# A graph kernel whose first pass gets 16 extra products of constants in each slot

## The chip, the cores and the metric

The kernel runs on one core of a Trainium2 chip. The metric is the device time of one execution in microseconds. The kernel before took 4850.95 us in the median of 3 runs (4839.13 to 4865.02).

## The reference

A graph of 12,500 nodes with 128 features and 212,500 edges, sorted by their destination, goes through two layers. The first layer sends typed messages: each edge carries its source's features through one of two weight matrices, and a node sums what arrives. The second layer is two hops of a normalised sum.

```python
h = jnp.maximum(_layernorm(x, axis=-1), 0.0)
# first layer: typed messages, summed by destination
m_data, m_ctrl = h[src] @ W_data.T + b_data, h[src] @ W_control.T + b_control
msg = jnp.where((edge_types == 0)[:, None], m_data, m_ctrl)
x = x + relu(segment_sum(msg, dst) + h @ W_self.T + b_self)
h = jnp.maximum(_layernorm(x, axis=-1), 0.0)
# second layer: two hops, norm = deg^-1/2[row] * deg^-1/2[col]
e = out = h
for _ in range(2):
    e = segment_sum(e[row] * norm[:, None], col)
    out = out + e
x = x + out / 3
```

## The kernel before, in words

After a preparation (some 140 us) in which the typed messages of all nodes are computed and stored as a table in the chip's memory, the kernel makes three passes over the edges, k = 0, 1, 2: the first layer, and the two hops. A pass is cut into slots, one for each group of 1024 edges (8 chunks of 128). The first pass has 208 slots. In each, for group o:

- GpSimd gathers the source rows of the group, 8 indirect DMAs into one of four buffers `rows` (L863). It waits until the group four places back has been summed (`summed`).
- VectorE makes the one-hot matrix `hot` of the destinations (L1499), two groups ahead.
- TensorE (`sum_group`) waits for `rows_landed`, `hot_ready` and `added` (group o - 2), multiplies rows by one-hot into one of the two banks of `sums_bank`, 80 columns (L1079), and counts the edges in the same bank, columns 128 to 207 (L1087). The last product raises `summed`.
- VectorE (`add_group`) adds the bank into `sums` and the counts into `degrees` (L1514, L1517) and raises `added`.

The first pass also builds, for the first 7,680 nodes, a dense table of edge counts that the hops use in place of gathers. This is done in "cells" of four nodes: 1920 cells in 480 quads, spread over slots 24 to 205. For a quad VectorE makes two one-hot operands (L1547, L1550) in one of two buffers; TensorE (`make_cells`) multiplies them, one product of 392 columns for each of the four cells, into one of three banks of `wide` (L1150); ScalarE casts each to 8 bits (L990); SyncE stores the finished strips (L756). `strip_hot_ready`, `strip_made` and `strip_kept` are the semaphores between them.

In some slots a batch of 512 nodes is closed: TensorE turns its degrees and its sums (L1099, L1106), counts the edges ahead of each cell (L1158, L1160) and turns fetched cell data (L1167).

Each engine runs its own list of instructions in the order in which its block of code writes them. For TensorE a slot of the first pass is `sum_group(i)`, the quads of the slot, then the turns. In the two hops TensorE multiplies the dense table (L1188) and sums the groups of the remaining edges.

Of the kernel before, what the change touches and what calls it, by code (L numbers as in the profile page):

```python
# [5 lines left out]
P = 128  # L6
# [33 lines left out]
DENSE_SLOTS = 80  # L40
LEAD_TILES = 3
LEAD_AT_ONCE = 3
CELL_START = 24
CELL_END = 206
CELL_BATCHES = 3
# [11 lines left out]
BF16 = mybir.dt.bfloat16  # L57
# [20 lines left out]
def gnn_kernel(nc, x, src, dst, edge_type, w_data, b_data, w_control, b_control, w_self, b_self, out):  # L78
# [156 lines left out]
    with ExitStack() as ctx:  # L235
# [92 lines left out]
        identity = sbuf("identity", [P])  # L328

        before_cell = sbuf("before_cell", [NODE_BLOCKS, P])  # L330
# [37 lines left out]
        sums_bank = bank("sums_bank", 2)  # L368
# [56 lines left out]
        added = semaphore("added")  # L425
# [95 lines left out]
        def steps_at(k, i):  # L521

            if i >= slots_of(k) and k < HOPS:
                first = (i - slots_of(k)) * LEAD_AT_ONCE
                return [step_number(k + 1, j) for j in range(first, min(first + LEAD_AT_ONCE, lead_steps[k + 1]))]
# [498 lines left out]
        def _(pe):  # L1024
# [86 lines left out]
            with pe.If(flag > 0):  # L1111
                for k in range(HOPS + 1):
# [12 lines left out]
                    for s in range(total):  # L1125
                        if k == 0:
                            turn_degrees(s, all_degrees[:, s * BATCH:s * BATCH + held(s) * P], (s, 0, 0))
                        n = k * total + s
                        turn_sums(n, s, all_sums[:, s * BATCH:s * BATCH + held(s) * P], n)
                pe.nop()  # L1130
            with pe.Else():
                def sum_group(o):
# [8 lines left out]
                        last = count_edges(o % 2, size_of(group), hot[:, slot, :, :], WINDOW)  # L1141
                    last.then_inc(summed, 1)

                def make_cells(quad):
                    pe.wait_ge(strip_hot_ready, quad + 1)
                    for w in range(QUAD):
                        nth = quad * QUAD + w
                        if nth >= CELL_BANKS:
                            pe.wait_ge(strip_kept, nth - CELL_BANKS + 1)
                        pe.matmul(wide[:, nth % CELL_BANKS, 0:real_blocks * CELL], quad_low[quad % 2][:, w, :], quad_hot[quad % 2][:, w, :],  # L1150
                                  start=True, stop=True).then_inc(strip_made, 1)
# [41 lines left out]
                for k in range(HOPS + 1):  # L1193
                    for i in range(slots_of(k) + LAST):
                        if i < slots_of(k):
                            sum_group(first_of[k] + i)
                        if k == 0 and i < groups:
                            for quad in quads_of_slot(i):
                                make_cells(quad)
                        elif k and i < hop_groups:  # L1200
                            for number in steps_at(k, i):
                                dense_step(number)
                        turning = event_at(k, i - 2)
                        if turning and not is_dense(k, turning[1]):
                            n, s = turning
                            r = turn_of[k, s]
                            j = next(first_cut[k] + j for j, (_, cut) in enumerate(cuts[k]) if cut == s)
                            pe.wait_ge(cut_made, j + 1)
                            if k == 0:
                                turn_degrees(s, degrees[j % 2], small_reads(i, degree_slot))  # L1210
                            before = event_of[turns[r - 1][0]][turns[r - 1][1]] + 1 if r else 0
                            turn_sums(r, s, sums[:, j % 2, :], before)
                        if k == 0 and i in place_slot:
                            place_cells(batch_of_slot(place_slot, i), small_reads(i, place_slot))
                        if k == 0 and i in cells_turn_slot:
                            turn_cells(batch_of_slot(cells_turn_slot, i), small_reads(i, cells_turn_slot))
                        if i >= slots_of(k):
                            for number in steps_at(k, i):
                                dense_step(number)
# [428 lines left out]
```

## Time and profile before

| | |
|---|---|
| median of 3 runs | 4850.95 us |
| profiled execution | 4842.59 us |
| its span, first to last instruction | 4840.8 us |
| mean granted TensorE clock | 0.728 of full |
| TensorE busy (products) | 3663.3 us, 76% |
| TensorE weight loads | 3001.0 us, 62% |
| GpSimd | 2869.0 us, 59% |
| ScalarE | 2307.7 us, 48% |
| VectorE | 1959.6 us, 40% |

The span is the time from the first to the last instruction of the profiled execution; 1.8 us lie around it. PE is TensorE's products, PEld its weight loads, DVE VectorE, ACT ScalarE, POOL GpSimd, SPq the DMA issues of SyncE. "idle before" names what ended the idle time of an engine; "issue" is time in which it waited for nothing that the profile shows, and "remote" is a release by a semaphore whose raiser the profile does not match.

### The profile page before, as it was taken

The page shows a single profiled execution, that of the slowest core. Times are in us where ns is not written, and L with a number is a line of the kernel's source. Part 1 is how long each engine was busy: PE and PEld are TensorE (multiplying, and loading weights), DVE is VectorE, ACT ScalarE, POOL GpSimd, SP SyncE. Part 2 cuts the span into 40 slices and gives each one's busy share as a digit, 9 for nine tenths or more (in the row PEclk, how much of TensorE's full clock was granted, in tenths as well). Part 3 has the DMA queues.
Part 4 walks back from the last instruction along what each step waited for, and adds up shares of the span by engine and source line. Part 5 has one row for each costly group of instructions (what it writes and reads, how often), then busy time and mean ns, then how long its engine had stood idle before and what let it go on. Part 6 is the DMA issues. An engine that isn't in the chain of part 4 may idle for free. (4 is left out here: it accounts for less than half of the span.)

```text
span 4840.8 us, 59773 instructions
## 1 busy us (share of the span) xinstructions
PE 3663.3 (76%) x22243; PEld 3001.0 (62%) x22243; DVE 1959.6 (40%) x3213; ACT 2307.7 (48%) x3075; POOL 2869.0 (59%) x3055
## 2 busy tenths in 40 slices
PE   7345766677667767666767699898897789998898
PEld 4334444444444444434444688888887688888888
DVE  7213666666666667667666011111112111111111
ACT  4001433333333434334334566666666566666666
POOL 2666665666665666666664556655663565655654
PEclk9555555555555555555556799999998899999999
DMA  5222332323232323233233455555555455555554
GB/s 186 58 53 67 95 92 87 107 90 91 91 107 91 91 91 105 92 95 107 92 103 97 123 149 153 154 156 150 154 151 168 130 148 139 145 144 146 145 144 132
DMA packets 367258, 571.63 MB, mean 118 GB/s; under 512 B 66678, under 2 KB 308225, under 8 KB 359283
## 3 DMA queue, kind: packets, MB, share of 16 engines
q1 hardware_dynamic: 270435, 370.74, 24.4%
q0 software_dynamic: 95664, 196.60, 16.1%
q8 instruction: 180, 2.95, 0.3%
q14 instruction: 115, 0.94, 0.1%
q10 hardware_dynamic: 864, 0.39, 0.0%
HBM read 424.48 MB, written 142.99 MB: 117 GB/s over the span
## 5 line engine op out<-in xcount | busy, mean ns | idle before, releaser
L863 POOL DMA_INDIRECT rows<-typed_table,index x1661 | 1584.4, 954 | 953.6 <-issue 503.1
L863 POOL DMA_INDIRECT rows<-hop_table,index x1306 | 1246.4, 954 | 943.3 <-PE sums_bank L1079 471.2
L999 ACT CAST strip_ring<-stage 128x1792 fp32r<-128x1792 uint8 x840 | 1376.3, 1685 | 751.4 <-remote 384.2
L1188 PE MATMUL wide<-table_parts,strip_ring 128*128 128x256 f32 x11760 | 1567.2, 296 | 112.4 <-issue 60.2
L1188 PEld LDWEIGHTS wide<-table_parts,strip_ring 128*128 128x128 f32 x11760 | 1525.7, 204 | 130.6 <-issue 108.3
L990 ACT CAST stage<-wide 128x392 uint8<-128x392 f32 x1920 | 801.3, 502 | 1356.1 <-PE wide L1150 878.4
L1079 PE MATMUL sums_bank<-hot,rows 128*128 128x80 f32 x5934 | 1095.1, 347 | 291.4 <-issue 240.9
L1150 PE MATMUL wide<-stage 128*128 128x392 bf16 x1920 | 755.1, 490 | 671.6 <-ACT stage L990 309.8
L1079 PEld LDWEIGHTS sums_bank<-hot,rows 128*128 128x128 f32 x5934 | 1047.1, 263 | 328.7 <-issue 325.5
L1150 PEld LDWEIGHTS wide<-stage 128*128 128x128 bf16 x1920 | 185.6, 110 | 1196.7 <-ACT stage L990 525.2
L1550 DVE TENSOR_TENSOR stage<-count_up,stage 128x1568 bf16<-128x1568 f32 x480 | 851.3, 1773 | 0.0
L1514 DVE TENSOR_TENSOR sums<-sums_bank,sums 128x80 f32 x372 | 88.6, 238 | 1331.5 <-PE sums_bank L1079 874.2
L1547 DVE TENSOR_TENSOR stage<-count_up,stage 128x512 bf16<-128x512 f32 x480 | 325.2, 677 | 516.1 <-PE wide L1150 426.0
L1580 DVE TENSOR_REDUCE own_in<-wide 128x128 f32<-128x256 f32 x120 | 50.9, 425 | 693.2 <-remote 421.7
L1499 DVE TENSOR_TENSOR hot<-count_up,local 128x640 f32<-128x640 f32 x372 | 300.2, 808 | 0.6 <-issue 0.2
L1087 PE MATMUL sums_bank<-hot,one_short 128*1 128x80 bf16 x1661 | 143.6, 251 | 46.1 <-issue 46.0
L1087 PEld LDWEIGHTS sums_bank<-hot,one_short 128*1 128x1 bf16 x1661 | 95.3, 105 | 81.4 <-issue 53.9
L964 ACT ACTIVATE batch_spread<-batch_spread 128x8 f32<-128x8 f32 x25 | 5.6, 222 | 292.6 <-DVE batch_spread L1247 283.8
L1044 PE MATMUL wide<-stage,rows 128*128 128x384 f32 x196 | 76.5, 516 | 0.0
L1444 DVE TENSOR_TENSOR table_parts<-stage,table_parts 128x896 fp32r<-128x896 f32 x14 | 15.3, 1092 | 105.2 <-ACT table_parts L1004 97.5
L1433 DVE TENSOR_TENSOR scaled<-fresh,inv 128x512 f32<-128x512 f32 (+1 forms) x50 | 34.1, 682 | 37.3 <-ACT fresh L933 30.8
L1099 PEld LDWEIGHTS wide<-one,stage 1*128 1x128 f32 x196 | 43.1, 317 | 9.0 <-issue 8.7
(140 smaller groups left out, 936.4 us busy)
## 6 DMA issues: line engine op xcount, KB each, us to landing
stage<-strips SPq DMA_DIRECT2D x840, 224.0 KB
strips<-stage SPq DMA_DIRECT2D x60, 1568.0 KB
rows<-typed_table,index POOLq DMA_INDIRECT x1661
rows<-hop_table,index POOLq DMA_INDIRECT x1306
hop_table<-scaled SPq DMA_DIRECT2D x50, 256.0 KB
resid<-xin SPq DMA_DIRECT2D x50, 256.0 KB
xin<-resid SPq DMA_DIRECT2D x50, 256.0 KB
typed_table<-rows SPq DMA_DIRECT2D x49, 256.0 KB, 2.1
```

The costliest lines, as they stand in the source:

```text
L863: pool.indirect_dma_start(out=rows[:, o % RING, c, :], out_offset=None, in_=tables[k], in_offset=bass.IndirectOffsetOnAxis(ap=index[:, chu ...
L990: act.copy(count_strips[tile % 2][:, :, w * CELL:(w + 1) * CELL], wide[:, nth % CELL_BANKS, 0:real_blocks * CELL].rearrange("p (b n) -> p ...
L999: act.copy(strip_ring[:, number % STRIP_RING], counts_ring[place]).then_inc(strip_cast, 1)
L1044: last = pe.matmul(wide[:, i % 2 * PAIR + b, 0:KINDS * P], normed_t[i % 2][:, b * P:(b + 1) * P], w_all[:, :], start=True, stop=True)
L1079: last = pe.matmul(sums_bank[:, bank, 0:columns], rows[:, slot, c, :], hots[:, c, :], start=(c == 0), stop=(c == size - 1))
L1087: last = pe.matmul(sums_bank[0:1, bank, P:P + columns], one_short[:, 0:1], upper, start=(c == 0), stop=(c == size - 1))
L1150: pe.matmul(wide[:, nth % CELL_BANKS, 0:real_blocks * CELL], quad_low[quad % 2][:, w, :], quad_hot[quad % 2][:, w, :], start=True, stop=Tr ...
L1188: last = pe.matmul(wide[:, nth % 4, 0:PARTS * P], strip_ring[:, number % STRIP_RING, b - first, :], table_parts[:, b, :, :].rearrange("p n ...
L1499: dve.tensor_tensor(hot[:, slot, :, :], counting(CHUNKS, WINDOW), local[:, group * CHUNKS:(group + 1) * CHUNKS].unsqueeze(2).to_broadcast( ...
L1514: last = dve.tensor_tensor(into, sums_bank[:, o % 2, 0:WINDOW], into, ALU.add)
L1547: dve.tensor_tensor(quad_low[place], counting(QUAD, P), cell_low[:, cells].unsqueeze(2).to_broadcast([P, QUAD, P]), ALU.is_equal)
L1550: dve.tensor_tensor(quad_hot[place], counting(QUAD, columns), cell_key[:, cells].unsqueeze(2).to_broadcast([P, QUAD, columns]), ALU.is_equ ...
```

## The change

In each slot of the first pass TensorE runs 16 bf16 products of 256 columns. Their operands are constants reread as bf16 (the identity matrix and a table of thresholds). They write columns 256 to 511 of the bank of `sums_bank` that the current group does not use; nobody reads these columns. Before them TensorE waits until the group before has been added. The products stand behind the quads of the slot and ahead of its turns.

```diff
+FILL = 16
...
+                ones = identity[:, :].bitcast(BF16)[:, 0:P]
+                moved = before_cell[:, :, :].rearrange("p b n -> p (b n)").bitcast(BF16)
+
+                def fill(o):
+
+                    if o:
+                        pe.wait_ge(added, o)
+                    for _ in range(FILL):
+                        pe.matmul(sums_bank[:, (o + 1) % 2, 2 * P:4 * P], ones, moved[:, 0:2 * P], start=True, stop=True)
...
                         if k == 0 and i < groups:
                             for quad in quads_of_slot(i):
                                 make_cells(quad)
+                            fill(i)
                         elif k and i < hop_groups:
```

TensorE's list in two of the first slots that have cells, before: a slot is a group (L1079), its counts (L1087) and two or three quads (L1150, here three); the turns of a batch follow (L1099, L1106).

```order
L1079 MATMUL sums_bank<-hot,rows 128x80 x8
L1087 MATMUL sums_bank<-hot,one_short 1x80 x8
L1150 MATMUL wide<-stage 128x392 x12
L1079 MATMUL sums_bank<-hot,rows 128x80 x8
L1087 MATMUL sums_bank<-hot,one_short 1x80 x8
L1150 MATMUL wide<-stage 128x392 x12
L1099 MATMUL wide<-one,stage 128x1 x4
L1106 MATMUL turned_bank<-identity,sums 128x128 x4
```

The same place in the changed kernel, where lines up to this one are numbered 1 higher and those behind the new function 12 higher; L1154 are the new products.

```order
L1080 MATMUL sums_bank<-hot,rows 128x80 x8
L1088 MATMUL sums_bank<-hot,one_short 1x80 x8
L1162 MATMUL wide<-stage 128x392 x12
L1154 MATMUL sums_bank<-before_cell,identity 128x256 x16
L1080 MATMUL sums_bank<-hot,rows 128x80 x8
L1088 MATMUL sums_bank<-hot,one_short 1x80 x8
L1162 MATMUL wide<-stage 128x392 x12
L1154 MATMUL sums_bank<-before_cell,identity 128x256 x16
L1100 MATMUL wide<-one,stage 128x1 x4
L1107 MATMUL turned_bank<-identity,sums 128x128 x4
```

Nothing changes places; 16 products are put between the quads of a slot and whatever came next on TensorE. The other engines' lists are as before.

## Rows read from the trace of the kernel before

**Rows 1.** Busy times, and TensorE's clock in 40 slices, from the page.
```profile
PE 3663.3 (76%) x22243; PEld 3001.0 (62%) x22243; DVE 1959.6 (40%) x3213; ACT 2307.7 (48%) x3075; POOL 2869.0 (59%) x3055
...
PEclk9555555555555555555556799999998899999999
```

**Rows 2.** Windows: span; PE, PEld, DVE, ACT, POOL busy (x); clock; DMA share; GB/s.
```profile
144.00:440.00 296.00, 138.85 (x681) 120.13 (x681) 53.08 (x144) 8.25 (x20) 198.48 (x210) 0.50 0.21 53
500.00:2500.00 2000.00, 1387.15 (x6145) 879.84 (x6142) 1335.78 (x1933) 773.70 (x1856) 1263.01 (x1329) 0.56 0.31 96
2724.00:4840.00 2116.00, 1864.17 (x14197) 1818.10 (x14195) 316.32 (x626) 1355.91 (x835) 1216.17 (x1274) 0.93 0.53 147
```

**Rows 3.** Groups of lines, 500 to 2500 us: busy, mean, idle before.
```profile
L863 POOL DMA_INDIRECT rows<-typed_table,index x1316 | 1250.8, 950 | 734.7 <-issue 405.0 <-remote 186.5 <-PE sums_bank L1087 143.1
...
L990 ACT CAST stage<-wide 128x392 uint8<-128x392 f32 x1736 | 725.0, 502 | 1190.2 <-PE wide L1150 776.9 <-remote 301.1 <-issue 110.3
...
L1514 DVE TENSOR_TENSOR sums<-sums_bank,sums 128x80 f32 x165 | 38.7, 234 | 130.3 <-remote 103.0 <-PE sums_bank L1087 14.5 <-issue 12.7
```

**Rows 4.** TensorE's wait for rows in L1138, 500 to 2500 us (min/median/max ns).
```profile
L1138 PEldq EVENT_SEMAPHORE  x164: 51/51/51, 503.0 to 2487.8; - x164
```

**Rows 5.** Timeline of one slot: start us, us, engine line op out<-in xcount.
```profile
1205.49 3.54 PE L1079 MATMUL sums_bank<-hot,rows 128*128 128x80 f32 x16
...
1209.58 1.16 PE L1150 MATMUL wide<-stage 128*128 128x392 bf16 x3
...
1213.53 3.21 ACT L990 CAST stage<-wide 128x392 uint8<-128x392 f32 x8 [7.23 <-remote]
...
1216.07 1.86 PE L1099 MATMUL wide<-one,stage 1*128 1x1 f32 x8
...
1217.86 1.12 PE L1106 MATMUL turned_bank<-identity,sums 128*128 128x128 f32 x4
...
1240.26 0.67 DVE L1547 TENSOR_TENSOR stage<-count_up,stage 128x512 bf16<-128x512 f32 x1
...
1242.56 0.67 DVE L1547 TENSOR_TENSOR stage<-count_up,stage 128x512 bf16<-128x512 f32 x1
```

**Rows 6.** Timeline, TensorE: a group and L1188 products at the full clock.
```profile
705.69 1.91 PE L1079 MATMUL sums_bank<-hot,rows 128*128 128x80 f32 x16
707.52 0.45 PE L1087 MATMUL sums_bank<-hot,one_short 128*1 128x80 bf16 x8
...
3117.12 5.08 PE L1188 MATMUL wide<-table_parts,strip_ring 128*128 128x256 f32 x41 [0.44 <-issue]
```

**Rows 7.** Timeline: TensorE at 231 us, and ScalarE's casts at 1530 us.
```profile
231.60 0.49 PE L1079 MATMUL sums_bank<-hot,rows 128*128 128x80 f32 x1 [0.42 <-issue]
232.29 0.50 PE L1079 MATMUL sums_bank<-hot,rows 128*128 128x80 f32 x1 [0.20 <-issue]
...
1530.91 0.49 ACT L990 CAST stage<-wide 128x392 uint8<-128x392 f32 x1 [0.17 <-issue]
1533.01 0.49 ACT L990 CAST stage<-wide 128x392 uint8<-128x392 f32 x1 [1.62 <-PE wide L1150]
1535.12 0.49 ACT L990 CAST stage<-wide 128x392 uint8<-128x392 f32 x1 [1.62 <-PE wide L1150]
...
1543.54 0.49 ACT L990 CAST stage<-wide 128x392 uint8<-128x392 f32 x1 [0.91 <-remote]
```

**Rows 8.** Queue q8, 500 to 2500 us, then the hops: packets, MB, share.
```profile
q8 instruction: 51, 0.84, 0.2%
...
q8 instruction: 112, 1.84, 0.4%
```

**Rows 9.** Timeline at 3103 us, and the window 3102 to 3104 us.
```profile
3102.99 0.33 PE L1079 MATMUL sums_bank<-hot,rows 128*128 128x80 f32 x1 [0.18 <-issue]
3103.69 1.62 PE L1079 MATMUL sums_bank<-hot,rows 128*128 128x80 f32 x8 [0.38 <-issue]
...
3102.00:3104.00 2.00, 1.18 (x7) 0.91 (x7) 0.25 (x1) 0.19 (x1) 0.02 (x1) 1.00 0.53 148
```

## The prediction

> **What bounds the kernel now.** I read the busy table with its slices first, then a windows table that cuts the program into its stages, then the groups of lines of the middle stage, then stretches of the timeline. The change touches only the first pass. The slices [rows 1] show TensorE's clock at 0.5 of full through the left half, the first pass, and at 0.8 to 0.9 in the two hops. Because the chain that ended last is a handful of steps at the end of the program, it says nothing about the first pass; the waits inside the slots do.
>
> From 500 to 2500 us VectorE added 165 groups (L1514) [rows 3], so a slot takes 2000 / 165 = 12.1 us. TensorE's mean clock there is 0.56 [rows 2], which is full speed for about 0.12 of the time and half speed for the rest. Who leads the slot?
> - GpSimd needs 950 ns for a gather and some 0.31 us to issue it (405.0 / 1316) (L863) [rows 3], 10.1 us for the eight of a slot; 2.0 us are left in which it waits for others. It is ahead of TensorE.
> - TensorE waits for gathered rows at the semaphore of L1138. In 164 slots that wait was never longer than its own 51 ns [rows 4]. So the rows are always there, and GpSimd does not lead.
> - VectorE is busy 67% and ScalarE 39% [rows 2]; of the 1190 us that ScalarE sat idle before its cell casts, 777 ended with a cell product of TensorE (L990) [rows 3].
> So TensorE leads, handing over to ScalarE and VectorE while it makes cells. A slot by its rows [rows 5]: from the first group product at 1205.49 to the first cell product at 1209.58 are 4.1 us; eight cells go at ScalarE's pace, 3.21 us; a third quad, which 0.64 of the slots have (480 quads in 182 slots, 2.64 each), comes one VectorE pair later, 2.30 us (L1547 at 1240.26 and 1242.56). That is 4.1 + 3.2 + 0.64 x 2.3 = 8.8 us. The turns of a batch, 1.9 + 1.1 us for the one shown (L1099, L1106), and other small work of that size come about once in five slots: 0.6. The sum is 9.4 us, and 2.7 us of the 12.1 are missing.
>
> **Where the missing 2.7 us are.** In some stretches TensorE's instructions come singly: eight casts of single cells on ScalarE start from 1530.91 to 1543.54, the first three at 1530.91, 1533.01 and 1535.12 [rows 7]. Their distances are three times 0.70 us, and 12.63 us over all seven is 18 times 0.70; 0.40 is normal. The same 0.70 stands between plain group products at 231.60 and 232.29 us [rows 7]. I take this as TensorE being short of instructions. The instruction queue q8 moved 51 packets of 16 KB in these 2000 us [rows 8], one for 12,287 / 51 = 241 records of products and weight loads [rows 2], one in 3.2 slots. So the 2.7 us are 8.7 us per packet, and the stretch shown fits that: its last seven steps take 12.6 us, which would be 2.8 at 0.40, or 5.1 with one wait for a VectorE pair. This is an inference, and the rival below drops it.
>
> **The change part by part.** It removes nothing and adds to each of 208 slots one wait and 16 products of 256 columns, behind the cells and ahead of the turns and the next group. In the trace each product has a weight load beside it (counts of PE and PEld agree, also for L1087, whose weights never change), so 32 records.
>
> 1. The wait for `added`. VectorE adds group o - 1 before it makes this slot's quads, and TensorE has needed those quads already; in slots without cells the addition had the 4.1 us of the next group's products. It costs nothing. Behind it in TensorE's queue stand the turns and the next group. If VectorE were late, the price would be the fraction of a us between two of its rows.
>
> 2. The fill at half clock. The trace has no product of 256 bf16 columns. Three cell products of 392 columns take 1.16 us with the last lasting about 0.5, as ends are modelled [rows 5], so they start 0.33 us apart, 0.83 ns per column: 0.213 us for 256, 3.4 us for 16. At full clock half of that, 1.7 us; the nearest row, 41 products of 256 columns in 5.08 us (0.124 each) [rows 6], gives 2.0. I take 1.8. Nothing hides it: it stands on the engine that leads. VectorE and ScalarE cannot use the time to get ahead, since two quad buffers and three banks hold them.
>
> 3. What the clock gives back. At full clock the group's products take 1.91 us and the counts follow 1.83 after the start, 2.1 us in all instead of 4.1 [rows 6]. Cells are paced by ScalarE and VectorE and gain at most 0.2 us at a hand-over; turns halve, 0.3. The group at 705.69 us lies in this pass [rows 6], so the clock rises here now and then already. With the fill, cells, fill and group are one dense block, so I expect a rise in nearly every slot and a fall back in the cell phase that waits for others. I choose a mean clock of 0.78, between 0.56 and the hops' 0.93 [rows 2]: high for 0.56 of the time. Fill 0.44 x 3.4 + 0.56 x 1.8 = 2.5; group (0.56 - 0.12) x 2.0 = -0.9; the rest -0.2. Net +1.4 us a slot. Ends: clock unchanged, +3.4; clock always full, 1.8 - 1.8 - 0.4 = -0.4.
>
> The Trainium skill, "TensorE: Matmul & The Clock Gate", section on the HAM clock gate, has the array at 1.2 GHz by default and at 2.4 GHz once it is kept busy. The trace bears out both levels; yet it also has 69% busy at a clock of 0.56 in this pass. By that rule taken alone the clock would be full and item 3 would stand at its lower end.
>
> 4. More instructions. A slot has 12,287 / 165 = 74.5 records now and 106.5 after, 1.43 times. If a packet costs 8.7 us as before, 2.7 us a slot become 3.9. Some of that time runs beside a fuller array queue, so I take +1.0. Ends: 0, if the stretches don't follow the count of instructions, and +1.2.
>
> The Trainium skill, "Runtime: NRT & Kernel Launch", section "Instruction fetch mechanics", says that an engine streams its instructions in 16 KiB blocks of 256 and that crossing into the next is mostly hidden. The packet size agrees; the 0.70 us steps do not look hidden. By that rule item 4 is nothing, which is the first rival's sum.
>
> 5. The 24 slots ahead of the first cells. Here 210 gathers in 296 us [rows 2] make 11.3 us a slot, near GpSimd's 10.1, and TensorE's 4.1 + 3.4 = 7.5 us would fit under it. Only the slow stretches grow: 1.2 us over GpSimd's pace, with 52 records a slot becoming 84, is +0.75 x 24, some 20 us. Ends 0 and 80 (all of the fill). The two hops have the same instructions as before: nothing.
>
> Sum: (1.4 + 1.0) x 182 = 437, + 20 = 457 us. On the profiled execution's 4842.6 (4840.8 of span and 1.8 around it) this gives 5300 us; the median of the runs shown, 4851, lies 8 us above and I leave it out.
>
> **Rivals.**
> - *Stretches follow time, not instructions.* A packet's delay is then a matter of the memory queues, as many per ms as before. For it: the hops read 112 packets in 2116 us [rows 8], more than twice as many per us, and TensorE is still busy 88% [rows 2]. Against: before the cells, without any strip traffic, the same 0.70 steps stand. Price 1.4 x 182 = +255: 5100 us.
> - *The clock does not rise*, since each stretch breaks the dense work. Against it is the group at 705.69 us, at full clock without any fill [rows 6]. (3.4 + 1.0) x 182 + 20 = +820: 5660 us.
> - *The other side: faster.* The clock goes to full and stays; group -1.8, rest -0.4, fill +1.8, and the stretches turn out to belong to the low clock, as their rarity in the hops suggests, and lose half, -1.3. That is -1.7 x 182 = -310: 4530 us. It decides the sign once the mean clock in the pass is above about 0.9 and a packet costs less than some 6 us. Against: group products start 0.70 us apart at 3102.99 and 3103.69 us as well, where the clock is full [rows 9], so the step isn't the low clock's; and the cells, more than half of a slot, are paced by others, so the clock has reason to fall.
> - *Covered.* If GpSimd led, the fill would fit in TensorE's waits: 4843. The 51 ns of [rows 4] speak against it.
> That the fill isn't executed can be left out: its products write a bank and are ordinary instructions.
>
> **How the numbers follow.** Forecast 0.53; stretches by time 0.22; clock stays low 0.08; faster 0.12; covered 0.05. The first three are slower: 0.83. What a measurement of this kernel can tell from no change is about 0.5%, 24 us; within it only the covered case, 0.05; faster 0.12. The range leaves out the faster and the covered case and most of the 5660: from 4920 (the first rival with a clock nearer to full, +0.4 a slot) to 5500 (the forecast with item 3 at a clock near 0.65 and item 4 at its end, 3.6 x 182). The forecast's own range is 5180 to 5420.
>
> **What would show it.** A group of 16 x 208 = 3328 products of 256 bf16 columns, 0.21 us apart where the clock is low, 0.11 to 0.12 where it is high. In 500 to 2500 us: a mean clock of 0.7 to 0.85, 138 additions instead of 165 (14.5 us a slot), about 61 packets in q8, GpSimd's idle time up by about 2.4 us a slot, the wait at L1139 still 51 ns. Group products at 1.91 us in over half of the slots. A first pass that is no longer than before, or waits for rows at L1139, would prove the forecast wrong; equal packets per us with 13.5 us a slot would speak for the first rival.

## The result, and the profile after

On the chip where both were timed, the changed kernel took 4900.54 us (median of 5, 4884.38 to 4909.82) and the kernel before 4848.99 us (median of 5, 4839.13 to 4865.02): ratio 1.0101, 95% interval 1.0070 to 1.0132. It is slower, as forecast, by 52 us and not by 457, and lies under the forecast's range of 4920 to 5500 us. Between the two profiled executions, which the rows below come from, the difference is 42 us. The first pass alone carries it: its last addition ends 44 us later than before (2694.3 us against 2650.3), and the hops after it take 2188 us against 2191.

The page: busy times, and TensorE's clock in 40 slices.

```profile
PE 3800.3 (78%) x25571; PEld 3084.0 (63%) x25571; DVE 1953.5 (40%) x3213; ACT 2295.4 (47%) x3075; POOL 2877.1 (59%) x3055
...
PEclk9666877777777787777778899999998899999999
```

The windows of [rows 2], the first from 140 us here: span; PE, PEld, DVE, ACT, POOL busy (x); clock; DMA share; GB/s.

```profile
140.00:440.00 300.00, 181.03 (x1090) 138.28 (x1091) 54.78 (x145) 8.54 (x20) 199.99 (x211) 0.65 0.21 53
500.00:2500.00 2000.00, 1444.25 (x8629) 912.14 (x8628) 1304.71 (x1892) 744.26 (x1819) 1245.67 (x1305) 0.77 0.31 94
2724.00:4840.00 2116.00, 1855.28 (x13989) 1813.77 (x13990) 307.54 (x607) 1349.64 (x829) 1231.29 (x1289) 0.92 0.53 147
```

The groups of lines that answer to [rows 3], with the new products (L1154), 500 to 2500 us.

```profile
L864 POOL DMA_INDIRECT rows<-typed_table,index x1292 | 1233.5, 955 | 750.7 <-issue 393.0 <-PE sums_bank L1088 223.4 <-remote 134.4
L991 ACT CAST stage<-wide 128x392 uint8<-128x392 f32 x1705 | 698.1, 510 | 1222.4 <-PE wide L1162 750.9 <-remote 396.9 <-issue 74.2
L1154 PE MATMUL sums_bank<-before_cell,identity 128*128 128x256 bf16 x2576 | 469.2, 360 | 0.0
L1527 DVE TENSOR_TENSOR sums<-sums_bank,sums 128x80 f32 x161 | 37.8, 235 | 130.2 <-PE sums_bank L1088 60.1 <-remote 56.8 <-issue 13.3
```

The wait for rows, and queue q8 in the same 2000 us.

```profile
L1139 PEldq EVENT_SEMAPHORE  x161: 51/51/51, 504.2 to 2487.3; - x161
```

```profile
q8 instruction: 70, 1.15, 0.2%
```

The clock rose from 0.56 [rows 2] to 0.77, almost the 0.78 that was forecast. The additions fell only from 165 [rows 3] to 161, not to 138, and q8 moved 70 packets instead of 51 [rows 8], one for 247 records of products and weight loads where it was one for 241. Over the whole program the change adds 6656 records and 26 packets (206 instead of 180), one for 256. The timeline of two slots shows what the clock does.

```profile
1209.01 2.77 PE L1154 MATMUL sums_bank<-before_cell,identity 128*128 128x256 bf16 x16
1211.62 1.91 PE L1080 MATMUL sums_bank<-hot,rows 128*128 128x80 f32 x16
1213.46 0.45 PE L1088 MATMUL sums_bank<-hot,one_short 128*1 128x80 bf16 x8
1213.85 0.67 PE L1162 MATMUL wide<-stage 128*128 128x392 bf16 x3
...
1233.92 3.62 PE L1154 MATMUL sums_bank<-before_cell,identity 128*128 128x256 bf16 x16
1237.33 2.27 PE L1080 MATMUL sums_bank<-hot,rows 128*128 128x80 f32 x16
```

The fill begins at half speed and ends at full; the group behind it takes 1.91 us, where [rows 5] had 3.54. The products themselves start 0.213 or 0.109 us apart.

I also cut each of the 182 slots with cells by ScalarE's cell casts: "cells" is from the first to the last cast of a slot, "between" from the last cast to the first of the next slot (turns, fill and group lie there). Slots of three quads last 5.2 us in cells when nothing disturbs them; over 8.5 us I call the cell phase long. Before: between 6.33, cells 5.81, 12.14 together, 37 long phases. After: between 7.64, cells 4.78, 12.42 together, 12 long phases. So 1.31 us came in where the fill stands, as item 3 had it (+1.4), but 1.03 us left the cells, where item 4 had expected more stretches.

### The profile page after: what moved, and what is told of

It is laid out like the page before. It is cut to its first block and busy times, and to the rows that moved or that the text cites. A ratio compares the mean times of both kernels' runs of the same rounds, so it can differ in the third digit from the quotient of the medians.

```text
span 4882.4 us, 66429 instructions
## 1 busy us (share of the span) xinstructions
PE 3800.3 (78%) x25571; PEld 3084.0 (63%) x25571; DVE 1953.5 (40%) x3213; ACT 2295.4 (47%) x3075; POOL 2877.1 (59%) x3055
## 5 line engine op out<-in xcount | busy, mean ns | idle before, releaser
L991 ACT CAST stage<-wide 128x392 uint8<-128x392 f32 x1920 | 786.7, 510 | 1396.6 <-PE wide L1162 855.8
L1162 PE MATMUL wide<-stage 128*128 128x392 bf16 x1920 | 653.3, 418 | 619.4 <-ACT stage L991 304.3
L1080 PE MATMUL sums_bank<-hot,rows 128*128 128x80 f32 x5934 | 836.3, 287 | 226.1 <-issue 223.2
L1080 PEld LDWEIGHTS sums_bank<-hot,rows 128*128 128x128 f32 x5934 | 790.0, 206 | 267.0 <-issue 260.2
L1162 PEld LDWEIGHTS wide<-stage 128*128 128x128 bf16 x1920 | 173.7, 104 | 1054.4 <-ACT stage L991 536.7
L1154 PE MATMUL sums_bank<-before_cell,identity 128*128 128x256 bf16 x3328 | 612.9, 359 | 52.5 <-issue 47.8
L1154 PEld LDWEIGHTS sums_bank<-before_cell,identity 128*128 128x128 bf16 x3328 | 423.9, 128 | 215.2 <-issue 81.0
L1088 PE MATMUL sums_bank<-hot,one_short 128*1 128x80 bf16 x1661 | 105.4, 204 | 32.3 <-issue 32.0
L1088 PEld LDWEIGHTS sums_bank<-hot,one_short 128*1 128x1 bf16 x1661 | 68.1, 85 | 53.4 <-issue 35.4
```

What stands on the lines that cost most here:

```text
L991: act.copy(count_strips[tile % 2][:, :, w * CELL:(w + 1) * CELL], wide[:, nth % CELL_BANKS, 0:real_blocks * CELL].rearrange("p (b n) -> p ...
L1080: last = pe.matmul(sums_bank[:, bank, 0:columns], rows[:, slot, c, :], hots[:, c, :], start=(c == 0), stop=(c == size - 1))
L1088: last = pe.matmul(sums_bank[0:1, bank, P:P + columns], one_short[:, 0:1], upper, start=(c == 0), stop=(c == size - 1))
L1154: pe.matmul(sums_bank[:, (o + 1) % 2, 2 * P:4 * P], ones, moved[:, 0:2 * P], start=True, stop=True)
```

## The experiments

The question after the result was where item 4's price had gone. A "stretch" is a part of the program in which TensorE's operations come in steps of 0.70 us. The first expectations weigh two theories: the forecast's, that the stretches follow the count of TensorE's instructions (theory 1), and that they come from the gathers (theory 2). Those that followed, A, B and C, are each told in the expectation that uses them; B is not the same in all of them.

The kernels ran in five sets, and in each the kernel before ran beside them on the same chip: 4996, 4995, 4008, 4008 and 4972 us. The third and fourth were in another condition than the rest: there no cell phase was long, and no two neighbouring products of groups start more than 0.6 us apart in the whole program. In the kernel before on the first chip 314 pairs do, 92 in the first pass and 222 in the hops. It isn't a matter of the piece of silicon, as the fourth and the fifth set ran on one chip. "Under stretches" and "without" below mean these two conditions; ratios are to the kernel before of the same set. Slots are means in us over the profiled execution; of the kernel before there is only the profile of the first chip, so a slot of another chip is set against it only roughly: pool_pause and width_before, whose times are those of the kernel before on their chips within 0.3%, have slots of 12.43 and 12.37. A difference of 0.3 us to its 12.14 can thus be the chip's. The ratios don't have this fault.

| kernel | ratio (95%) | slot | between | cells | long |
|---|---|---|---|---|---|
| *under stretches* | | | | | |
| before (first chip) | 1 | 12.14 | 6.33 | 5.81 | 37 |
| changed (first chip) | 1.0101 (1.0070-1.0132) | 12.42 | 7.64 | 4.78 | 12 |
| after_again | 1.0041 (1.0012-1.0070) | 12.44 | 7.80 | 4.63 | 9 |
| small16 | 1.0077 (1.0060-1.0094) | 12.43 | 7.70 | 4.74 | 8 |
| split32 | 1.0202 (1.0185-1.0219) | 12.72 | 8.41 | 4.30 | 0 |
| fill32_c | 1.0216 (1.0171-1.0261) | 12.76 | 8.52 | 4.24 | 0 |
| inside | 1.0394 (1.0338-1.0449) | 13.54 | 5.63 | 7.91 | 49 |
| pool_pause | 1.0002 (0.9987-1.0017) | 12.43 | 7.36 | 5.07 | 10 |
| width_before | 0.9999 (0.9972-1.0026) | 12.37 | 6.43 | 5.94 | 34 |
| two_halves_c | 0.9976 (0.9960-0.9991) | 12.21 | 6.92 | 5.29 | 26 |
| half_gather | 0.8673 (0.8657-0.8688) | 9.38 | 4.96 | 4.42 | 0 |
| half_after | 0.8826 (0.8778-0.8874) | 9.84 | 5.61 | 4.23 | 0 |
| *without* | | | | | |
| after_third | 1.0002 (0.9992-1.0011) | 10.19 | 5.96 | 4.22 | 0 |
| two_halves | 0.9995 (0.9985-1.0004) | 10.20 | 5.83 | 4.37 | 0 |
| fill32 | 1.0467 (1.0450-1.0485) | 11.21 | 7.03 | 4.19 | 0 |
| six | 0.9469 (0.9453-0.9485) | 9.42 | 4.99 | 4.43 | 0 |
| half_small | 0.9556 (0.9539-0.9572) | 9.92 | 5.57 | 4.35 | 0 |
| half_split | 0.9611 (0.9595-0.9627) | 9.92 | 5.70 | 4.22 | 0 |

### Does the price follow instructions, columns or the clock?

small16 makes each of the 16 products 8 columns wide; split32 has 32 of 128.

```diff
-                        pe.matmul(sums_bank[:, (o + 1) % 2, 2 * P:4 * P], ones, moved[:, 0:2 * P], start=True, stop=True)
+                        pe.matmul(sums_bank[:, (o + 1) % 2, 2 * P:2 * P + 8], ones, moved[:, 0:8], start=True, stop=True)
```

```diff
-FILL = 16
+FILL = 32
-                        pe.matmul(sums_bank[:, (o + 1) % 2, 2 * P:4 * P], ones, moved[:, 0:2 * P], start=True, stop=True)
+                        pe.matmul(sums_bank[:, (o + 1) % 2, 2 * P:3 * P], ones, moved[:, 0:P], start=True, stop=True)
```

> The changed kernel with 16 products of 8 columns in place of 256: the same 32 extra records in a slot, almost no columns. Theory 1 (the stretches in which TensorE's operations come 0.70 us apart follow the count of its instructions, item 4 of the prediction): the clock stays near 0.56, 16 weight loads of 128 columns at the low clock cost about 1.7 us and the stretches 1.0, so 2.7 x 182 = +490 us on before, 5340 us, and again some 70 packets in q8 from 500 to 2500 us. Theory 2 (the stretches go with GpSimd: they come where it has gathered for over 10 us without a pause, and a longer slot on TensorE gives it pauses): the 1.7 us are mostly taken from the stretches, under +0.7 us a slot, below 4980 us.

> 32 products of 128 columns in place of 16 of 256: the same columns, 32 more records a slot than the changed kernel. Theory 1: +1.2 us a slot on the changed kernel, 5120 us. Theory 2: the count is nothing, the weight loads are hidden, 4900 us within 25. Both: clock near 0.77, about 90 packets in q8 from 500 to 2500 us.

> The changed kernel once more, so that its ratio is known on the chip of the experiments: 1.01 as on the first chip; beside small16 (1.0077) and split32 (1.0202) it says whether columns or instructions set the price. All theories expect 1.01.

The windows, 500 to 2500 us, of small16 and then of split32:

```profile
500.00:2500.00 2000.00, 1456.53 (x8547) 945.08 (x8547) 1294.00 (x1874) 735.69 (x1801) 1229.99 (x1292) 0.54 0.30 94
```

```profile
500.00:2500.00 2000.00, 1475.83 (x10868) 1002.59 (x10869) 1268.20 (x1846) 715.02 (x1762) 1204.61 (x1265) 0.76 0.29 92
```

One block of small16's products in its timeline:

```profile
1007.15 0.61 PE L1154 MATMUL sums_bank<-before_cell,identity 128*128 128x8 bf16 x16
```

small16 brings the 32 records of the change and nearly none of its columns. The clock stays at 0.54, a block takes 0.6 us where its expectation had 1.7, and the kernel is 36 us slower than before on its chip, 0.2 us a slot. Theory 1 asked for 490 us. So item 4's price per record (+1.0 us a slot) is refuted. The change itself cost 52 us on the first chip and, in after_again, 23 us on another (1.0041, where all theories expected 1.01), so small16 costs about as much as the change: the higher clock of the changed kernel brings no time beyond what pays for its own columns. split32, with twice the records of the change, is 104 us over the kernel before on its chip and has a slot 0.3 us longer than the change's, a third of what item 4 would have it. That is too much for theory 2 as well, which gave it the time of the changed kernel within 25 us.

### Are the missing 2.7 us TensorE's own?

half_gather is the kernel before with every second chunk gathered in the first pass; the other chunks are summed from what the buffer held. half_after is the changed kernel with the same edit. In both, as in six below, the count of landed rows for which TensorE waits is lowered to match; that part of the edit is left out here.

```diff
-                for c in range(size_of(group)):
+                for c in range(0, size_of(group), 1 if k else 2):
```

> The kernel before, with only every second chunk's rows gathered in the first pass (the rest of the work is the same, its values are not): GpSimd's part of a slot falls from 10.1 to 5.0 us. Theory 1: GpSimd does not lead, slots stay at 12.1 us, time within 30 us of before. Theory 2: GpSimd never gathers for over 10 us without a pause, the stretches vanish, slots with cells take about 9.4 us: -2.7 x 182 = -490 us and some -100 in the slots ahead of the cells, 4250 us.

> In the first pass only every second chunk of a group is gathered (4 of 8 gathers; the other chunks are summed from old rows), and the 16 products of 256 columns stand in each slot. Only the comparison with half_gather counts, which had no 0.70 us stretches, a slot of 9.36 us and a mean clock of 0.73. Theory A (the stretches come with the gathers, and they gave back what the 16 products cost): with no stretch left to shrink, the products cost their whole net price. Clock up to about 0.9, fill 0.2 x 3.4 + 0.8 x 1.8 = 2.1 us, group -0.7, so +1.4 us a slot, slot 10.7 us, about +250 us: ratio to before 0.92 instead of 0.867. Theory B (TensorE has room of its own in each slot for the 16 products, whatever GpSimd does): slot 9.4 to 9.7 us, ratio 0.87 to 0.88.

The windows 500 to 1900 us of half_gather and of half_after:

```profile
500.00:1900.00 1400.00, 1082.94 (x5553) 693.36 (x5554) 1204.27 (x1739) 683.37 (x1675) 583.10 (x608) 0.68 0.29 96
```

```profile
500.00:1900.00 1400.00, 1131.51 (x7533) 739.74 (x7532) 1139.39 (x1662) 646.43 (x1593) 550.37 (x577) 0.87 0.28 92
```

With half the gathers the slot is 9.38 us, the 9.4 of the forecast's sum, and no cell phase is long, although TensorE's instructions are the same. In the kernel before, 199 of the 1920 cell casts start more than 1 us after both the record of their product and the cast ahead of them have ended (463 us in all); in half_gather one does. So the missing 2.7 us hang on GpSimd's gathers.

The stretches are not gone from the whole program, though. In the hops, which gather as before, half_gather has 199 pairs of group products more than 0.6 us apart (222 in the kernel before), and in the slots ahead of the cells it still has 21 (83 before). There the four gathers of a slot follow those of the last with little pause, 93 of them from 140 to 280 us, and the 0.70 us steps stand beside them:

```profile
206.02 0.29 PE L1079 MATMUL sums_bank<-hot,rows 128*128 128x80 f32 x1 [0.35 <-issue]
206.71 0.52 PE L1079 MATMUL sums_bank<-hot,rows 128*128 128x80 f32 x2 [0.40 <-issue]
```

With half the gathers the changed kernel's 16 products cost 0.46 us a slot, not the 1.4 of theory A: "between" grows by 0.65 and the cells shrink by 0.19 at the higher clock. That was the surprise of this pair. The slot of 9.84 us and the ratio of 0.8826 lie just over what theory B gave.

half_small and half_split put the products of small16 and split32 on half_gather.

> half_gather with the 16 products of 8 columns in each slot: their price where there are no stretches. With small16 they took 0.45 us from the first start to the last, left the clock at 0.54, and the slot grew by 0.3 us. Theory A (what they cost is partly taken out of the stretches): here the slot grows by 0.6 us or more, ratio 0.888 to 0.895. Theory B (the price is the same with and without stretches): slot +0.3 us, ratio 0.878 to 0.882. In either case it is above 0.883 of half_after only if the higher clock of the 256 columns pays for their own time.

> half_gather with 32 products of 128 columns in each slot: the columns of half_after, 64 records instead of 32. If columns and clock alone set the price, ratio 0.88 as half_after (0.8826). If each record has a price of its own (32 more a slot), up to +0.6 us a slot more, ratio 0.90 or above. split32 stood 0.016 above after_again with the same edit under all gathers.

Both have a slot of 9.92 us, 0.54 above half_gather's: for 32 products of 128 columns the same as for 16 of 8, and 0.08 more than for 16 of 256, so a record has next to no price of its own. They ran without stretches and half_gather under them, so the ratios that were written for them don't apply; but the slot of TensorE's own work is the same in both conditions (9.38, and 9.42 in six). For half_small the 0.54 lies between theory B's 0.3 and theory A's 0.6, nearer to A.

### What in the gathers is it?

width_before fetches half of each row; pool_pause adds three chained memsets on GpSimd behind each group; two_halves and two_halves_c (the same kernel) let GpSimd wait in mid-group for the last cell product of the slot; six and six_again gather six chunks of eight.

```diff
-                        out=rows[:, o % RING, c, :], out_offset=None, in_=tables[k],
+                        out=rows[:, o % RING, c, 0:P if k else P // 2], out_offset=None, in_=tables[k],
```

```diff
...
                     gather(o)
+                    if k == 0:
+                        for n in range(3):
+                            pool.memset(pause[:, :], 0.0).then_inc(paused, 1)
+                            pool.wait_ge(paused, (o - EARLY) * 3 + n + 1)
```

```diff
                 for c in range(size_of(group)):
+                    if c == 4 and k == 0 and o >= EARLY and len(quads_of_slot(o - EARLY)):
+                        pool.wait_ge(strip_made, QUAD * (quads_of_slot(o - EARLY)[-1] + 1))
```

```diff
-                for c in range(size_of(group)):
+                for c in range(size_of(group) if k else min(6, size_of(group))):
```

> The kernel before, but each gather of the first pass fetches only the first 64 of 128 floats of a row: as many gathers and as many rows, half the bytes (the sums of the other 64 features come from old data). If the 0.70 us stretches come from the bytes that the gathers move, they go as in half_gather: slot 9.4 us, ratio 0.87 to 0.90. If they come from GpSimd's issuing of gathers or from the number of row transfers, nothing changes: slot 12.1 us, ratio 0.99 to 1.00.

> The kernel before with three small memsets on GpSimd, one after the other, behind each group of gathers of the first pass, about 1 us in all, which fits under the 2.0 us in which it waits. Theory 1: no change, 4850 within 25. Theory 2: every run of gathers ends after 10 us, so fewer stretches: -0.5 to -1.5 us a slot, 4580 to 4760 us. If a pause of 1 us is too short to count, no change either, and the run says only that.

> On a chip with stretches, theory A (unbroken gathering slows TensorE): slot 10.3 to 11.5 us, ratio 0.93 to 0.98; if the number of gathers counts or neither: 12.1 us and 1.00. On a chip without stretches 1.000 again.

> The kernel before with 6 of the 8 gathers of each group of the first pass (the last two chunks are summed from old rows). A slot of TensorE's own work is 9.4 us (half_gather) and 12.1 with all eight gathers. Theory A (TensorE is slowed only while GpSimd gathers for more than some 8 to 10 us without a pause, and comes free when GpSimd has to wait): six gathers take 7.6 us, each slot leaves a pause, the stretches go: slot 9.4 to 9.8 us, early slots about 8, ratio 0.88 to 0.90. Theory B (each gather beyond the fourth costs TensorE its share): half of the 2.7 us stay, slot 10.8 us, ratio 0.93 to 0.94.

Queue q0 from 500 to 2500 us, in the kernel before and then in width_before (packets, MB, share):

```profile
q0 software_dynamic: 42695, 87.97, 16.9%
```

```profile
q0 software_dynamic: 42057, 44.22, 11.1%
```

Half the bytes in as many packets change nothing, so it isn't the bytes. What made me think of unbroken gathering were places like this in the kernel before, ahead of the first cells, in the timeline: TensorE's rows, then GpSimd's, then VectorE's.

```profile
194.29 0.22 PE L1087 MATMUL sums_bank<-hot,one_short 128*1 128x80 bf16 x1 [0.43 <-issue]
196.39 0.36 PE L1087 MATMUL sums_bank<-hot,one_short 128*1 128x80 bf16 x3 [1.88 <-issue]
199.19 0.29 PE L1087 MATMUL sums_bank<-hot,one_short 128*1 128x80 bf16 x2 [2.44 <-issue]
211.78 0.47 PE L1079 MATMUL sums_bank<-hot,rows 128*128 128x80 f32 x1 [12.30 <-DVE stage L1517]
...
206.69 0.94 POOL L863 DMA_INDIRECT rows<-typed_table,index  x1 [0.30 <-issue]
211.37 0.94 POOL L863 DMA_INDIRECT rows<-typed_table,index  x1 [3.73 <-remote]
...
211.30 0.24 DVE L1514 TENSOR_TENSOR sums<-sums_bank,sums 128x80 f32 x1 [24.89 <-remote]
```

TensorE's products come in multiples of 0.70 us while GpSimd gathers without a pause; the addition, which needs only this group's products, starts 12 us after the last of them has its record, and 3.7 us after GpSimd had to stop for want of a free buffer. In the 24 slots ahead of the cells the addition starts 13.0 us after the last count product's record has ended in the mean of the kernel before, 3.6 us in half_gather, and 0.2 us in two_halves, without stretches.

But cutting the gathers did not help. pool_pause took the long cell phases from 37 to 10, and has 1.03 us more in "between" than the kernel before has on the first chip. two_halves_c did the same more weakly, and won 14 us in the medians (0.9976), not the 100 to 350 of theory A. Its windows row, 500 to 2000 us, is nearly that of the kernel before, which has a clock of 0.55 and 1386 instructions of ScalarE there:

```profile
500.00:2000.00 1500.00, 1017.87 (x4633) 648.68 (x4632) 993.96 (x1446) 573.73 (x1382) 942.54 (x990) 0.58 0.29 95
```

It was a weak test. The wait came into effect 44 times in these 1500 us, some 120 slots, for 100 us in all, and GpSimd's waits for other engines add up to 264 us where the kernel before has 252: the pauses were moved and not lengthened.

```profile
POOL rows L865 <- PE wide L1152: 100.3, 44, 5.0
```

So unbroken gathering is not ruled out as what the stretches need. That it isn't enough is shown by after_third below, where GpSimd gathers without a pause from 500 to 2000 us and no stretch comes.

six fell on the condition without stretches, twice (six_again: 0.9495, slot 9.35, the same picture), so whether six gathers would still bring stretches under the other condition isn't known; two_halves and its repetition there (1.0002) had nothing to cut.

> The kernel before, where GpSimd waits after the fourth gather of a group until the last cell product of the current slot, so that its ten us of gathers are cut in two with idle time between; nothing else changes and nothing is left out. Theory A (unbroken gathering slows TensorE): shorter stretches, slot 10.3 to 11.5 us, ratio 0.93 to 0.98, faster than both kernels. Theory B (only the number of gathers counts): slot 12.1 us, ratio 1.00. If the wait makes GpSimd late: TensorE waits for rows_landed and the ratio is over 1.

> two_halves once more: on the chip without stretches it had nothing to cut (ratio 0.9995, slot 10.2 us, GpSimd without a pause). On a chip with stretches, theory A (unbroken gathering slows TensorE) gives a slot of 10.3 to 11.5 us and 0.93 to 0.98; theory B and C (the number of gathers counts) 12.1 us and 1.00.

> Six of eight gathers in the first pass once more. On the chip without stretches its slot was 9.42 us, TensorE's own, as in half_gather. On a chip with stretches: theory A 9.4 to 9.8 us and 0.88 to 0.90; theory B (stretch time in proportion to the gathers beyond four) 10.8 us and 0.93 to 0.94; in proportion to all gathers is already excluded by half_gather.

### The change without stretches, and a double dose

> The changed kernel beside the kernel before once more, since chips differ: before took 4851, 4996 and 4995 us on three and 4008 us on a fourth, where no 0.70 us stretch slowed the first pass and its slot was 10.2 us, GpSimd's own pace. On a chip with stretches (before near 5000): ratio 1.004 to 1.01 as so far. On a chip without them (before near 4008): TensorE's own slot with the 16 products is 9.8 us (half_after), under GpSimd's 10.1, so the products are hidden: ratio 1.000.

> The changed kernel with 32 instead of 16 products of 256 columns per slot. 16 of them had a clean price of 0.45 us a slot, since the clock rose from 0.68 to 0.87 (half_gather to half_after). 32 at nearly full clock: 16 x 0.109 = 1.7 us more, little left for the clock to give back. Stretches constant per slot (theory C): slot 12.4 + 1.7 = 14.1 us on a chip with stretches, ratio 1.06 to 1.07; if they are still absorbed (theory A): slot under 13.3, ratio under 1.04. On a chip without stretches: TensorE's slot is 11.5, over GpSimd's 10.1, ratio 1.05 to 1.07.

> fill32 on another chip. Without stretches it took 11.2 us a slot and 1.047. On a chip with stretches (before near 5000 us), theory C (stretches cost 2.6 us per slot whatever TensorE does there): 11.2 + 2.6 = 13.8 us a slot, ratio 1.06; theory A (added work is taken out of the stretches, because a longer slot gives GpSimd more idle time): under 13.0 us, ratio under 1.035.

Four fences: the window 500 to 2000 us of after_third, GpSimd's waits there (us, times, longest), and the same window of fill32 without and of fill32_c under stretches:

```profile
500.00:2000.00 1500.00, 1211.67 (x7874) 791.45 (x7872) 1187.49 (x1730) 673.39 (x1660) 1137.14 (x1192) 0.85 0.37 115
```

```profile
POOL rows L864 <- issue: 357.7, 1174, 0.3
POOL rows L864 <- PE sums_bank L1088: 1.8, 6, 0.3
```

```profile
500.00:2000.00 1500.00, 1281.18 (x9293) 897.20 (x9291) 1076.45 (x1565) 607.33 (x1498) 1036.95 (x1088) 0.91 0.34 105
```

```profile
500.00:2000.00 1500.00, 1218.58 (x8181) 823.85 (x8180) 946.11 (x1376) 533.20 (x1316) 896.68 (x945) 0.85 0.28 92
```

Without stretches GpSimd waits 1.8 us in 1500: it leads, at 10.2 us a slot, and TensorE's 9.84 fit under it. The changed kernel then costs nothing (1.0002), as written. 32 products put TensorE at 11.21 us, over GpSimd, and cost 1.0467, a little under the 1.05 to 1.07 written for them. The second 16 add 1.37 us to TensorE's own slot, the first 16 added 0.46: the clock had 0.68 to 0.87 to give for the first and 0.04 for the second. Under stretches the same 32 cost 1.0216 only, 12.76 us a slot, where a constant 2.6 us on top would make 13.8 and 1.06. That was theory C; it falls.

### The fill ahead of the third quad

```diff
-                            for quad in quads_of_slot(i):
-                                make_cells(quad)
-                            fill(i)
+                            for n, quad in enumerate(quads_of_slot(i)):
+                                if n == 2:
+                                    fill(i)
+                                make_cells(quad)
```

> The changed kernel with the 16 products placed ahead of the third quad of a slot (in slots with three quads only, 0.64 of them) instead of behind the cells; there TensorE waits for VectorE's pair. Theory A (the price of the products is mostly taken out of the stretches): ratio 0.99 to 1.01, clock in 500 to 2500 us about 0.70, the time between the last cell of a slot and the first of the next shorter than in the changed kernel, the cells longer. If the products' cost were paid where they stand, hiding them would make it as fast as before or faster (0.98 to 1.00).

It is the worst of all that were tried, 1.0394, though it has fewer products (only slots with three quads have them). Three-quad cell phases last 8.2 us in the median instead of 5.2, so TensorE's wait there does not hide them, and 49 are long. The expectation of 0.99 to 1.01 was wrong. The long ones last 15.7 us in the mean, and 8.0 us of these lie between the eighth cast and the ninth, where the fill stands. The fill's products take the same 2.5 to 3 us in all 116 slots; but in the 49 the ninth cell's cast starts 7.8 us after the record of its product has ended, and in the other 67 0.6 us after. So most of the length is a stretch's. Why one comes just there stays open. In the first of them the product's record stands at 476.77 us:

```profile
475.02 1.91 PE L1154 MATMUL sums_bank<-before_cell,identity 128*128 128x256 bf16 x16
476.77 0.66 PE L1162 MATMUL wide<-stage 128*128 128x392 bf16 x3
483.93 0.49 ACT L991 CAST stage<-wide 128x392 uint8<-128x392 f32 x1 [7.97 <-issue]
```

Of the kernels that do all the work none beat the one before by more than two_halves_c's 0.24%.

## Why the prediction was right in sign and wrong in size

Set TensorE's own slot (from the kernels with half the gathers, and fill32) beside the slot under stretches. As the slots come from several chips, a rest holds to some 0.2 or 0.3 us:

| products in a slot | own | under stretches | rest |
|---|---|---|---|
| none | 9.38 | 12.14 | 2.76 |
| 16 of 256 columns | 9.84 | 12.42 | 2.58 |
| 16 of 8 | 9.92 | 12.43 | 2.51 |
| 32 of 128 | 9.92 | 12.72 | 2.80 |
| 32 of 256 | 11.21 | 12.76 | 1.55 |

- **Item 4 is the step that failed in kind.** It charged 8.7 us per packet of q8 and so +1.0 us a slot. Records and packets went up by 1.4 (packets 51 to 70), and the rest did not go up with them: it is 2.58 after, 2.76 before. Halving the gathers takes it away in the slots with cells, with the instructions unchanged. The coincidence of 2.7 us a slot with one packet per 3.2 slots was read as a cause. The rule of the Trainium skill, "Runtime: NRT & Kernel Launch", section "Instruction fetch mechanics", that crossing between blocks of instructions is mostly hidden, stood against item 4 in the prediction; small16 agrees with it.
- **Item 3 had its mechanism right and its size too high.** The clock came as chosen (0.77), the fill took 2.75 us a slot (blocks of 2.59 us between first and last start, and the step to what follows), the group's 16 products 1.77 us from first to last start instead of 2.94. But where no stretch is in play the slot grows by 0.46 us, not 1.4. Cut at the starts of TensorE's records, half_after has over half_gather +2.27 us for the fill (item 3: +2.5) and -0.93 for the group (item 3: -0.9). All the rest is -0.9: -0.36 from the counts to the first cell, -0.34 in the cells, -0.19 for the turns and the step ahead of the fill. Item 3 put "the rest" at -0.2, and this is the term that was mis-sized. Part of it is in slots in which TensorE waits for VectorE longer than the fill lasts: in half_gather and half_after alike 18 of the 133 slots without turns have 9.0 to 11.1 us between cells. That "nothing hides it" was too strong there. These are the waits of half_gather and half_after, 500 to 1900 us (us, times, longest); they did not shrink in sum by more than 16 us:

```profile
PEld wide L1150 <- DVE stage L1550: 238.0, 144, 8.8
```

```profile
PEld wide L1162 <- DVE stage L1563: 222.5, 135, 7.0
```

- **The stretches move and give way.** In the changed kernel the cells lost 1.03 us and "between" took 1.31. With half the gathers the same edit changes them by -0.19 and +0.65. So 0.8 us less of stretch lies in the cells and 0.7 more between them, about as much in sum. The late casts show it too: 124 of the changed kernel's start over 1 us late (323 us), 199 of the kernel before (463 us). With more work the sum falls as well: 32 products lengthen TensorE's own slot by 1.83 us and the real one by 0.62. A slot of eight gathers lasted 12.1 to 12.8 us under stretches whatever TensorE had of its own between 9.4 and 11.2; only work inside the cells (13.5) broke out of that.
- **Item 5** (+20 us in the 24 slots ahead of the cells): they took 11.6 us each and 11.8 before, 4 us less in all. Its upper end of 80 us was far off. Items 1 and 2 held: the wait and the half-clock distances (0.213 us) are as forecast.
- **What bounds.** "GpSimd does not lead" was right by the waits, and yet too simple. Its 10.1 us a slot, not TensorE's 9.4, is the floor without stretches, as *covered* had it, a case that got 0.05; and TensorE's lag of 2.7 us exists only with all gathers. Halving them in a thought, as half_gather did on the chip, would have put the question. The rival "stretches follow time" had the right doubt, that they don't follow instructions, and kept item 3's 1.4; it gave 5100.
- The sum in its own terms: +0.46 (own) - 0.18 (rest) = +0.28 us a slot, x 182 = 51, -4 early, and -6 because the first addition came 6 us sooner in this execution: 41 us, against 44 at the end of the first pass. The rest is what is left over when the own slot is taken off the slot, so the sum says where the time lies and proves nothing about it.

Open stays what a stretch is. The runs show that in the slots with cells it goes away when four of the eight gathers are left out, that ahead of the cells some of it stays even then, that it doesn't depend on the bytes of the gathers, is not cured by pauses of 1 us or by the cut of two_halves_c, and is absent in some conditions of a chip. Whether it needs gathering without a pause isn't decided, nor why it gives way when TensorE has more work. They do not show how a gather holds TensorE up, nor whether TensorE or its signals are late.

## What to carry to other kernels

A stall that is put down to a cause by a matching average should be tested by the count that would move it: here 16 small products, 32 records (no change in the stalls) and half of the gathers (stalls gone in the slots with cells) told in two runs what the trace could not. Where two engines are near each other (9.4 and 10.1 us), added work on one is paid only in part, and how much depends on the other: the same edit cost 1.0%, 0.4% or nothing. A higher granted clock is not time gained: small16 at 0.54 was about as fast as the change at 0.77.

## What the hardware showed that was not expected

- One chip ran the kernel before in 4007.56 us (19 runs, 4002.12 to 4012.59) in one set of runs and in 4972.06 us (13 runs, 4955.82 to 4984.72) in the next. The stretches came and went with it. The hops differ too: behind the last addition of the first pass come 2191 us in the kernel before on the first chip, 2319 in half_gather, and 1763 in six, all with the same instructions. The windows from 74 to 1050 us behind that addition, of the kernel before and then of six, have TensorE busy for 89% and for 97%:

```profile
2724.00:3700.00 976.00, 872.38 (x6699) 853.62 (x6697) 147.18 (x295) 634.41 (x390) 590.60 (x617) 0.94 0.55 153
```

```profile
2114.00:3090.00 976.00, 950.07 (x7943) 948.88 (x7943) 188.82 (x364) 785.59 (x476) 692.91 (x724) 0.98 0.66 186
```

  Both conditions were steady within a set.
- In a stretch TensorE's records run ahead of what the other engines see: 12 us between the last product's record at 199.19 and the addition that waited for it, and up to 25 us in other slots ahead of the cells. In two_halves, without stretches, it is 0.2 us in all of these slots.
- The records that the change adds to TensorE bring one instruction packet of q8 for 256 of them. The time in stretches did not grow with these packets.
